# Attention in one kernel of a larger program: exponents written back over their scores in PSUM, a ring of four pieces for the split probabilities, and another table of side jobs

## The reference, cut to what matters

```python
qkv = x @ W_qkv                       # 16 heads of 64
q, k = apply_rope(q), apply_rope(k)
dots = einsum('bhid,bhjd->bhij', q, k) * scale
dots = where(causal, neg, dots)       # row i sees keys 0..i
attn = softmax(dots, axis=-1)
out  = einsum('bhij,bhjd->bhid', attn, v)
out  = relu(out @ W_o1) @ W_o2        # then a layer norm with gamma
```

## Time and profile before

| | |
|---|---|
| median of 3 runs | 5949.6 us (5946.11 to 5954.65) |
| the profiled execution: its time, its span | 5942.21 us, 5940.3 us |
| attention heads, batch 0 and 1 (all turns with scores) | about 3420 to 4390 and 4545 to 5470 us |
| one MIDDLE turn, between the same instruction of two turns | 3799.94 to 3919.02, 119.08 us |
| PE, DVE, ACT, POOL busy in that turn | 104.51, 101.30, 81.65, 72.34 us |

### The profile page before, as it was taken

How to read it: one execution, slowest core, us unless ns; L and a number is a source line. 1 busy time by engine, 2 the same in 40 slices (tenths; PEclk the granted TensorE clock), 3 DMA queues, 4 the chain that set the end, 5 groups by cost and what they waited for, 6 DMA issues and landing times. The chain is left out here.

```text
span 5940.3 us, 81715 instructions
## 1 busy us (share of the span) xinstructions
PE 3936.9 (66%) x27691; PEld 2390.1 (40%) x27691; DVE 4405.1 (74%) x5229; ACT 2385.7 (40%) x3604; POOL 2650.9 (45%) x1626
## 2 busy tenths in 40 slices
PE   3976555444444545489495388888855888888395
PEld 2652111111111111156385155555633555556384
DVE  6873799999999999988301578888866888887301
ACT  1223432333333333212221166667743666667231
POOL 0211676676676776512202056655303646650202
PEclk9998655566666555599598599999977999999597
DMA  2000000000000000000254222222102212220254
GB/s 73 0 4 6 0 0 0 0 0 0 0 0 0 0 0 0 15 0 0 87 170 127 73 46 54 54 46 46 35 29 55 54 43 51 53 52 6 89 183 136
DMA packets 216325, 235.76 MB, mean 40 GB/s; under 512 B 61547, under 2 KB 181284, under 8 KB 214880
## 3 DMA queue, kind: packets, MB, share of 16 engines
q1 hardware_dynamic: 206304, 207.35, 13.1%
q0 software_dynamic: 8704, 24.35, 1.2%
q10 hardware_dynamic: 1024, 0.13, 0.0%
HBM read 116.95 MB, written 31.59 MB: 25 GB/s over the span
## 5 line engine op out<-in xcount | busy, mean ns | idle before, releaser
L971 PE MATMUL mix_scan_y<-mix_scan_hc,ident 128*128 128x512 f32 x512 | 476.9, 1086 | 957.1 <-DVE mix_scan_hc L904 957.1
L2040 DVE TENSOR_TENSOR att_b_prob_low<-att_b_prob,att_b_prob_high 128x1024 f16<-128x1024 f32 (+2 forms) x640 | 780.8, 1220 | 237.3 <-ACT att_b_prob_high L2002 223.7
L895 DVE TENSOR_TENSOR_SCAN mix_scan_h<-mix_scan_a_bar,mix_scan_state,mix_scan_dub 128x512 f32<-128x512 f32 x256 | 834.1, 3297 | 0.1
L2067 DVE TENSOR_REDUCE att_b_neg_max<-att_b_peek 128x1 f32<-128x1024 f32 (+7 forms) x768 | 684.3, 905 | 75.5 <-PE att_b_peek L1897 39.1
L2008 ACT ACTIVATE att_b_prob<-att_b_score,att_soft 128x1024 f32<-128x1024 f32 (+2 forms) x640 | 631.9, 987 | 169.6 <-PE att_b_score L1917 102.7
L852 ACT ACTIVATE mix_scan_a_bar<-mix_val,mix_A 128x512 f32 (+1 forms) x256 | 170.8, 714 | 1219.4 <-DVE mix_scan_h L895 1219.4
L971 PEld LDWEIGHTS mix_scan_y<-mix_scan_hc,ident 128*128 128x128 f32 x512 | 149.9, 323 | 1233.8 <-DVE mix_scan_hc L904 1102.0
L2002 ACT CAST att_b_prob_high<-att_b_prob 128x1024 f16<-128x1024 f32 (+2 forms) x640 | 587.9, 919 | 30.4 <-PE att_b_o L1945 13.1
L1941 PE MATMUL att_b_o<-att_b_vh,att_b_prob_high 128*128 128x65 f16 x4352 | 465.4, 195 | 179.4 <-DVE att_b_heads L2058 88.6
L1941 PEld LDWEIGHTS att_b_o<-att_b_vh,att_b_prob_high 128*128 128x128 f16 x4352 | 400.6, 98 | 306.3 <-DVE att_b_prob_low L2040 205.9
L816 POOL TENSOR_TENSOR mix_scan_dub<-mix_u,mix_scan_b_row 128x512 f32<-128x512 f32 x128 | 279.7, 2185 | 412.8 <-ACT mix_scan_b_row L856 412.8
(11 more groups left out here) (329 smaller groups left out, 9595.6 us busy)
## 6 DMA issues: line engine op xcount, KB each, us to landing
moe_w<-in_L_ffn_W_dram SPq DMA_DIRECT2D x64, 1024.0 KB, 8.1
att_b_crossed<-att_b_raw SPq DMA_DIRECT2D x512, 64.0 KB, 2.0
att_b_q_both<-att_b_halves SPq DMA_DIRECT2D x256, 64.0 KB, 2.0
att_b_k_twice<-att_b_halves SPq DMA_DIRECT2D x256, 64.0 KB, 2.0
moe_slots_in<-moe_route_zero SPq DMA_DIRECT2D x2, 4096.0 KB, 14.2
moe_exp_x<-moe_slots_in SPq DMA_DIRECT2D x32, 256.0 KB, 4.2
moe_slots_out<-moe_exp_y POOLq DMA_DIRECT2D x32, 256.0 KB, 6.5
att_b_k_low<-att_b_halves SPq DMA_DIRECT2D x128, 64.0 KB, 2.0
```

The costliest lines, as they stand in the source:

```text
L895: dve.tensor_tensor_scan(cols(hs, 0, m), cols(a_bar, b, m), cols(dub, b, m), state[:, at:at + 1], ALU.mult, ALU.add).then_inc(scanned, 1)
L971: done = pe.matmul(y_ps[m][:, :], ident[:, :], cols(hc, n % 2, m), start=(n == 0), stop=(n == S_N - 1))
L2040: dve.tensor_tensor(prob_low[:, at:at + width], prob[:, at:at + width], prob_high[:, at:at + width], ALU.subtract).then_inc(low_ready, 1)
L2067: last = dve.tensor_reduce(neg_max[:, first + col:first + col + 1], peek_ps[:, base:base + nb * P], AX.X, ALU.max, negate=True)
```

## The change

Four things. The f32 buffer `prob` is gone: `exponents` writes back into the PSUM slot it reads, and `high_part` and `low_part` read the exponents there. `scores(v)` therefore waits for `low_ready` of piece v-2 and no longer for `expd`; `exponents` waits for its scores alone. `prob_high` and `prob_low` become rings of four pieces. On ACT a step is now exponents(v), high_part(v), side job; on DVE it is maximum(v), low_part(v), take(v-2), side job. The table `SIDE` puts the qk jobs at steps 0, 3, 6, 9, 12, 15, 18, 21 (before: 0, 2, 4, 7, 9, 12, 14, 17), and moves some other jobs by a step or more.

```diff
-SIDE = {0: ("qk", 0, 1), 2: ("qk", 1, 1), 3: ("turn", 3, -1), 4: ("qk", 2, 1), 5: ("out", 6, -1), 6: ("out", 7, -1),
...
+SIDE = {0: ("qk", 0, 1), 3: ("qk", 1, 1), 4: ("turn", 3, -1), 5: ("out", 6, -1), 6: ("qk", 2, 1), 7: ("out", 7, -1),
+        9: ("qk", 3, 1), 12: ("qk", 4, 1), 15: ("qk", 5, 1), 16: ("mrow", 1, 0), 18: ("qk", 6, 1), 21: ("qk", 7, 1),
+        22: ("v", 0, 1), 23: ("v", 1, 1), 24: ("v", 2, 1), 25: ("turn", 0, 0), 26: ("out", 0, 0), 27: ("out", 1, 0),
+        28: ("v", 3, 1), 29: ("turn", 1, 0), 30: ("out", 2, 0), 31: ("out", 3, 0), 35: ("turn", 2, 0),
         36: ("mrow", 0, 1), 37: ("out", 4, 0), 38: ("out", 5, 0)}
...
-                wait_unless_first(pe, expd, piece(t, m - 1))
+                wait_unless_first(pe, low_ready, piece(t, m - 1))
...
-                    if has_piece(kind, v - 1):
-                        high_part(t, v - 1)
                     if has_piece(kind, v):
                         exponents(t, v)
+                        high_part(t, v)
...
-                act.copy(prob_high[:, at:at + width], prob[:, at:at + width]).then_inc(high_ready, 1)
+                act.copy(prob_high[:, to:to + width], score[m % 2][:, 0:width]).then_inc(high_ready, 1)
...
-                wait_unless_first(act, low_ready, piece(t, m - 1))
-                act.activation(prob[:, at:at + width], score[m % 2][:, 0:width], ACT.Exp, scale=soft[:, 0:1])\
-                    .then_inc(expd, 1)
+                act.activation(mine, mine, ACT.Exp, scale=soft[:, 0:1]).then_inc(expd, 1)
...
-                    if has_piece(kind, v - 1):
-                        low_part(t, v - 1)
-                    if v >= 2 and has_piece(kind, v - 2) or v < 2 and has_piece(kind, -1):
-                        take(t, b, v - 2)
                     peek_at = slot_at(kind, v)
                     if peek_at:
                         maximum(t, *peek_at)
+                    if has_piece(kind, v):
+                        low_part(t, v)
+                    if v >= 2 and has_piece(kind, v - 2) or v < 2 and has_piece(kind, -1):
+                        take(t, b, v - 2)
...
-                dve.tensor_tensor(prob_low[:, at:at + width], prob[:, at:at + width], prob_high[:, at:at + width],
+                dve.tensor_tensor(prob_low[:, to:to + width], score[m % 2][:, 0:width], prob_high[:, to:to + width],
```

More of the change, by code:

```diff
@@ L1553 @@
 LEAD = STEPS * 3 // 5
+RING = 4
 QK_JOBS, V_JOBS, TURN_JOBS, OUT_JOBS = 2 * CH, CH, CH, QT // 2
 BEFORE, FIRST, MIDDLE, LATE, LAST, AFTER = range(6)
-SIDE = {0: ("qk", 0, 1), 2: ("qk", 1, 1), 3: ("turn", 3, -1), 4: ("qk", 2, 1), 5: ("out", 6, -1), 6: ("out", 7, -1),
-        7: ("qk", 3, 1), 9: ("qk", 4, 1), 12: ("qk", 5, 1), 14: ("qk", 6, 1), 16: ("mrow", 1, 0), 17: ("qk", 7, 1),
-        19: ("v", 0, 1), 20: ("v", 1, 1), 21: ("v", 2, 1), 22: ("v", 3, 1), 25: ("turn", 0, 0), 26: ("out", 0, 0),
-        27: ("out", 1, 0), 29: ("turn", 1, 0), 30: ("out", 2, 0), 31: ("out", 3, 0), 35: ("turn", 2, 0),
+SIDE = {0: ("qk", 0, 1), 3: ("qk", 1, 1), 4: ("turn", 3, -1), 5: ("out", 6, -1), 6: ("qk", 2, 1), 7: ("out", 7, -1),
+        9: ("qk", 3, 1), 12: ("qk", 4, 1), 15: ("qk", 5, 1), 16: ("mrow", 1, 0), 18: ("qk", 6, 1), 21: ("qk", 7, 1),
+        22: ("v", 0, 1), 23: ("v", 1, 1), 24: ("v", 2, 1), 25: ("turn", 0, 0), 26: ("out", 0, 0), 27: ("out", 1, 0),
+        28: ("v", 3, 1), 29: ("turn", 1, 0), 30: ("out", 2, 0), 31: ("out", 3, 0), 35: ("turn", 2, 0),
         36: ("mrow", 0, 1), 37: ("out", 4, 0), 38: ("out", 5, 0)}
@@ L1630, in attention_heads @@
         v_cols = vh[:, :].rearrange("p (s e) -> p s e", e=COL)
-        prob = sb("prob", [P, 2 * SPAN])
-        prob_high, prob_low = sb("prob_high", [P, 2 * SPAN], F16), sb("prob_low", [P, 2 * SPAN], F16)
+        prob_high, prob_low = sb("prob_high", [P, RING * SPAN], F16), sb("prob_low", [P, RING * SPAN], F16)
         neg_max, max_row = sb("neg_max", [P, 2 * (QT + SB)]), sb("max_row", [QT, 2 * P], F16)
@@ L1936, in weigh @@
                 for k, at, i in blocks:
-                    at = slice(m % 2 * SPAN + at, m % 2 * SPAN + at + P)
+                    at = slice(m % RING * SPAN + at, m % RING * SPAN + at + P)
                     s = b * QT * 2 + k * 2 + h
@@ L1998, in high_part @@
             def high_part(t, m):
-                at, width = m % 2 * SPAN, width_of(m)
+                to, width = m % RING * SPAN, width_of(m)
                 act.wait_ge(expd, piece(t, m + 1))
-                wait_unless_first(act, p_done, piece(t, m - 1))
-                act.copy(prob_high[:, at:at + width], prob[:, at:at + width]).then_inc(high_ready, 1)
+                wait_unless_first(act, p_done, piece(t, m + 1 - RING))
+                act.copy(prob_high[:, to:to + width], score[m % 2][:, 0:width]).then_inc(high_ready, 1)
             def exponents(t, m):
-                at, width = m % 2 * SPAN, width_of(m)
+                mine = score[m % 2][:, 0:width_of(m)]
                 act.wait_ge(scored, piece(t, m + 1))
-                wait_unless_first(act, low_ready, piece(t, m - 1))
-                act.activation(prob[:, at:at + width], score[m % 2][:, 0:width], ACT.Exp, scale=soft[:, 0:1])\
-                    .then_inc(expd, 1)
+                act.activation(mine, mine, ACT.Exp, scale=soft[:, 0:1]).then_inc(expd, 1)
             in_turns(act, turn)
@@ L2034, in low_part @@
             def low_part(t, m):
-                at = m % 2 * SPAN
+                to = m % RING * SPAN
                 tiles = PIECES_S[m % NH][1]
@@ L2038, in low_part @@
                 dve.wait_ge(high_ready, piece(t, m + 1))
-                wait_unless_first(dve, p_done, piece(t, m - 1))
-                dve.tensor_tensor(prob_low[:, at:at + width], prob[:, at:at + width], prob_high[:, at:at + width],
+                wait_unless_first(dve, p_done, piece(t, m + 1 - RING))
+                dve.tensor_tensor(prob_low[:, to:to + width], score[m % 2][:, 0:width], prob_high[:, to:to + width],
                                   ALU.subtract).then_inc(low_ready, 1)
```

## The result

The changed kernel takes 6003.4 us (median of 4 runs) where the kernel before, on the same chip, takes 5947.9 (4 runs): ratio 1.0096, 95% interval [1.0079, 1.0114]. It is slower by 1%. The forecast was 5906 and the range ended at 5985, so both missed; "slower" had a chance of 0.23.

What follows compares the result with a forecast made beforehand. No single bound; in attention turns PE and DVE are both near their limits. A turn of 93.8 + 20.5 + 1.0 = 115.3 us against 119.08 gains 53 us over 14, less 10 in LAST turns: 5899, or 5906 against the median; range 5825 to 5985.

Steps and rivals of the forecast that it cites:

- Part one: DVE low parts reading PSUM lose no time beside POOL: 7.5 us a turn gone, DVE busy 93.8 us.
- price of the PSUM source: Rival: each of 640 low parts takes 0.065 us more from PSUM, +41 us, 5947, no change; chance 0.08.
- The blocking: Rival: low parts still contend with POOL despite the PSUM source, 105 us come back, 6011; chance 0.06.
- Part two: ACT makes the high part right behind its exponents, so low parts' 15.3 us a turn of waiting goes.
- part three: Moved take and longer-held score slots: DVE idle 20.5 us a turn, from chunk ends, qk jobs, other jobs and narrow pieces.
- 4.0 + 7.6: DVE idle a turn: 4.0 us at six qk jobs outside chunk ends, 7.6 at other jobs and narrow pieces.
- the stack: Later qk job 5, read by step 22's peek after rotation and six stacking DMAs: 1 us a turn, bounds 0 and 3.
- 5 us for a LAST turn: Loss in each of two LAST turns: four chunk ends at 1.1 us, held slot about nothing; 10 us together.
- the slot's chain of 2.2 us a step: LAST turn's end: scores, exponents, high and low part take 4.45 us over two steps, against ACT's 2.16 a step.
- Part four: Wider qk spacing in the table: ACT stops waiting for POOL, later job 5 costs 1 us a turn.
- PE gets no lead: Rival: scores come at the low part's pace, 9 us a turn more; 6032, half of it about 5970; chance 0.17.
- much faster: Rival: stalls overlap where PE is behind anyway, DVE idle 12 us a turn; 176 us gained, 5773; chance 0.17.

Runs made afterwards that it cites:

- e2: Changed kernel with DVE's take(v-2) moved ahead of maximum(v), new table kept; 0.9809 of the kernel before.
- e8: Kernel before with exponents written over their scores in PSUM and read there, scores waiting for the low part, old orders, rings and table; 0.9947 of the kernel before.
- e7: As e6, but scores wait for the exponents of two steps earlier instead of their low part; 1.0022 of the kernel before.
- e5: As e2, but buffers of high and low parts are rings of two instead of four; 5831.0 us, 0.9801 of the kernel before.
- e6: As e5, but exponents go to a two-slot SBUF buffer and are read there, scores still waiting for the low part; 5980.2 us, 1.0054 of the kernel before.

## Why the prediction was wrong

Part one was right. DVE's busy time was forecast at 93.8 us a turn and is 658.18 / 7 = 94.0. Low parts are 1218, 1084 and 548 ns in the mean, against the 1.22, 1.08 and 0.55 us that were asked for, and the longest of all 640 takes 1226 ns, where it took 2307. No price of the PSUM source shows: 1218 ns from PSUM stands beside 1.22 us quiet from SBUF, so that rival falls. The Trainium skill, "VectorE: DVE Perf Modes", section on the TRN2 errata, has a fixed term of 120 cycles for a PSUM source and 58 for SBUF; for this instruction the measurement doesn't show the difference.

The blocking is gone, and so that rival falls too. The rule of the Trainium skill, "SBUF — State Buffer", section "Who interferes with whom", holds in this case, on both engines: with one SBUF input instead of two, DVE's 1024-column low part went from 1408 to 1218 ns in the mean of the seven turns, and POOL's L1684 beside it from 1948 to 1488 ns.

Part two was right in what it removed: the low parts' wait for high parts went from 101.7 to 14.6 us in seven turns, and the longest is 0.5 us, the fraction of a microsecond that was asked for. Their sum, 2.1 us a turn, stood at nothing in the forecast.

**The step that failed is part three: the idle time of DVE that it adds up, with the late take in it, and after it the 5 us for a LAST turn.** The mechanism that it names, a gap behind each take, is there; the gap is larger than its price, and waits that it had at nothing stand beside it. The forecast turn was 115.3 us; it is 120.1 in the second batch. Item by item there, in us a turn:

- DVE busy: 94.0 for 93.8.
- Maxima waiting for peeks at the chunk ends, that is, the first maximum behind a take: 79.6 / 7 = 11.4, forecast 8.9. The 1.4 us of weigh, peek and landing were worked out at full clock. In the chunk end shown, PE had stood 2.51 us, ran the peek and what followed at half rate, and the gap became 1.94 us.
- All other maxima waiting for peeks: 80.4 / 7 = 11.5, forecast 4.0 + 7.6, and 1.0 for the stack. PE's peeks wait 0.5 for the stack (3.5 us in seven turns), which is within the 11.5.
- High parts 2.1, `vl` 0.4 and small gaps 0.7: forecast 0.

e2 gives the late take's whole price: 137.5 us in the 14 turns and 21.3 in the two LAST turns, 159 together, where the forecast has 14 x 8.9 + 8 x 1.1 = 133. So the take's price was 26 us short, a quarter of the miss; the sum below has the rest.

The larger mistake is what was not asked. I priced the take's new place by the gap that it opens on DVE, and never compared it with the same change with the take left where it was. By my own walk such a kernel had a turn of 115.3 - 8.9 = 106.4 us (e2 has 110.2 in the mean of 14), and I took the 8.9 for a detail of a change whose other parts won more. It was the whole of the gain: by e2 the rest of the change wins 9.4 us a turn, and the late take costs 9.8. Of PE I said that the peek and the side job queue behind its wait, and gave that wait no price of its own. It is 76.1 us in seven turns, against 38.7 before and none in e2's rows.

The LAST turns were put down at 5 us each and lost 21 and 22. There DVE has no blocking to get back, and two things cost, both seen alone: the held slot (e8: +3.3 and +6.1 in the halves) and the late take (changed kernel less e2: 7.6 and 3.2). Together they are 10.9 and 9.3 of the 11.7 and 10.7 us of the second batch. I had held the slot's chain of 2.2 us a step harmless beside ACT's 2.16. The chain was walked at full clock and without waits of the low part, which are 27.1 us in the second half against 12.4. e7, where the slot is free early and the take is first, still has 50.7 us there; which part of the new orders does that was not tried.

Part four was wrong in sign but small. The table gains 0.3 to 0.4%. It costs 5 to 7 us in each of the two preparations, which I had at nothing.

The sum: forecast -43 us, measured +62 in the span. Turns: 66 us worse than 14 x 115.3, of which 8 are because the one turn that I took as unit, 119.08, is shorter than the mean of before (119.8 and 119.5 in the two batches). Of the other 58, 13 are what the late take cost beyond its price, and 45 would have been missing with the take first too (14 x (110.2 - 106.4), less the 8); the waits that I had at nothing, 3.2 us a turn, come to as much. LAST turns: 33 worse, 12 of them the late take beyond its price. Ahead of the batches: 11 worse. Together 103 of the 105 us between the forecast 5899 and the profiled execution, 6004.3.

Of the rivals, "PE gets no lead" had the right side and, with the idle time of 26.1 us just past its point of 25.3, nearly the right size: 6003.4 lies between its 5970 and 6032. Its mechanism is not what happened in the preparing turns: scores wait for low parts 10.3 us there in seven turns. It is what happens in e8 (92.6 us) and, in part, in the LAST turn (3.1 and 6.4 us in its halves, where the kernel before has none). Of "much faster", two thirds of the 176 us was to be had, by leaving the take first: e5 is 118 us under the kernel before of its series, 5949.1.

The parts do not add. With the take first and the new table and ACT order, PSUM is worth 2.6% (e5 against e6), and in the orders of before 0.5% (e8). The new orders and table with the take first but the exponents in SBUF (e6, e7) are no gain at all, 1.005 and 1.002. ACT's new order and the low part in its own step were not run alone, so what each of them is worth stays open.

## What to carry to other kernels

When an instruction that frees a buffer moves within an in-order queue, price it from both sides: what waits for it on the other engine, and what its own engine can do until that engine has answered. Here the take wants its own place first and at least one instruction behind it that needs nothing from PE; and an instruction that feeds the next peek may not stand behind one that waits for a third engine. Price such a move against the same change without it, and do so again in the stages where the gain that pays for it doesn't occur.

## What the runs showed of the hardware

- The contention between DVE and POOL costs both. POOL's rotation instructions, seven turns, in e6 and then in the changed kernel:

```profile
L1685 POOL TENSOR_SCALAR att_b_halves<-att_b_raw 128x512 f16<-128x512 f32 x56 | 110.3, 1970 | 15.1 <-POOL att_b_raw L1682 13.3
L1681 POOL TENSOR_TENSOR att_b_crossed<-att_b_crossed,att_b_sin 128x512 f32<-128x512 f32 x56 | 94.4, 1685 | 0.0
```

```profile
L1684 POOL TENSOR_SCALAR att_b_halves<-att_b_raw 128x512 f16<-128x512 f32 x56 | 83.3, 1488 | 15.1 <-POOL att_b_raw L1681 13.3
...
L1680 POOL TENSOR_TENSOR att_b_crossed<-att_b_crossed,att_b_sin 128x512 f32<-128x512 f32 x56 | 70.9, 1266 | 0.0
```

  With one PSUM source in DVE's low part they take 1.49 and 1.27 us, with two SBUF sources 1.97 and 1.69. e5, which differs from e6 in the place of the exponents alone, has 1.49 and 1.27 too.
- ACT writing its exponents into the PSUM slot that it reads takes 1089 ns for 1024 columns, against 1115 to SBUF, and the f16 copy from PSUM 1012 against 1047.
- PE's granted clock can fall to 0.50 behind short waits within a busy stretch, as in the 3.13 us shown behind a wait of 2.51 us. In the seven turns of the changed kernel two full matmuls of the scores start 0.43 us apart behind twelve waits, eleven of them for a take and 1.69 to 2.67 us long; behind other waits of the same lengths they start 0.22 apart. In e2's seven turns there are three such places. For equal work PE is busy 728.8 us in the changed kernel's seven turns (mean granted clock 0.97) and 713.1 in e2's (0.98).
